# Attention and mixture of experts in one kernel: the experts' down products from one fp32 product to three float32r products of halves

## What is computed

```
xn  = layernorm(x)
out = x + attention(xn) + ffn(xn)

attention: 16 heads of 128, causal softmax, biases, output matrix, b_O
ffn:       x1 = xn + rotary_attention(rmsnorm(xn))      # 16 query heads, 4 key/value heads
           h  = rmsnorm(x1)
           p  = softmax(h @ gate.T); 4 of 32 experts by p + bias, their p made to sum to 1
           out = x1 + shared_expert(h) + sum over the chosen experts e of
                 w_e * ((silu(h @ weg[e]) * (h @ weu[e])) @ wed[e])
```

## Time and profile before

| what | value |
|---|---|
| median of 3 runs | 765.23 us (764.35 to 765.55) |
| profiled execution | 767.44 us |
| its span | 765.6 us |
| PE, DVE, ACT, POOL busy | 741.5, 543.1, 488.9, 476.4 us |

### The profile page before, as it was taken

How to read it: one execution, slowest core, us unless ns; L and a number is a source line. 1 busy time by engine, 2 the same in 40 slices (tenths; PEclk the granted TensorE clock), 3 DMA queues, 4 the chain that set the end, 5 groups by cost and what they waited for, 6 DMA issues and landing times. The chain is left out here.

```text
span 765.6 us, 14411 instructions
## 1 busy us (share of the span) xinstructions
PE 741.5 (97%) x4647; PEld 661.1 (86%) x4647; DVE 543.1 (71%) x1688; ACT 488.9 (64%) x1220; POOL 476.4 (62%) x550
## 2 busy tenths in 40 slices
PE   6799999999999999999989999999999999999997
PEld 3679898888889898989878989999989999999986
DVE  5888978797978887766698667555556565555574
ACT  3777777687777775677436665555656555666552
POOL 4757678686967685336355774466565856655553
PEclk9999999999999999999999999999999999999999
DMA  6001000000110099601002453476967876677634
GB/s 196 9 15 36 8 29 15 21 16 21 42 29 29 15 282 266 149 15 35 23 29 49 118 187 99 101 171 144 223 164 169 196 167 160 146 162 167 127 59 138
DMA packets 102691, 76.99 MB, mean 101 GB/s; under 512 B 6918, under 2 KB 101466, under 8 KB 102618
## 3 DMA queue, kind: packets, MB, share of 16 engines
q1 hardware_dynamic: 91426, 62.74, 29.4%
q0 software_dynamic: 10608, 12.61, 10.4%
q10 hardware_dynamic: 584, 0.73, 0.3%
HBM read 51.36 MB, written 24.69 MB: 99 GB/s over the span
## 5 line engine op out<-in xcount | busy, mean ns | idle before, releaser
L701 POOL TENSOR_SCALAR probs<-probs,inv_sum 128x128 f32<-128x128 f32 x240 | 141.2, 603 | 151.0 <-DVE inv_sum L1488 145.9
L1204 ACT ACTIVATE probs<-probs,neg_max 128x128 f32<-128x128 f32 (+3 forms) x256 | 143.0, 559 | 119.8 <-DVE neg_max L1482 118.6
L873 PE MATMUL s<-k_heads,q_heads 128*128 128x256 f32 (+2 forms) x576 | 137.9, 360 | 1.6 <-DVE neg_max L1482 1.2
L1482 DVE CUSTOM_DVE_ANT_0 probs<-s,mask 128x128 f32<-128x128 f32 (+3 forms) x256 | 120.0, 485 | 14.8 <-PE s L873 10.1
L763 POOL DMA_INDIRECT moe_sum_dram<-late,slot_tokens x63 | 99.2, 1574 | 40.9 <-ACT late L1292 27.8
L1497 DVE TENSOR_TENSOR probsT<-t,probsT 128x384 fp32r<-128x384 f32 (+2 forms) x192 | 101.2, 548 | 10.9 <-ACT probsT L1219 10.6
L1219 ACT ACTIVATE probsT<-t 128x384 fp32r<-128x384 f32 (+2 forms) x192 | 90.1, 487 | 17.9 <-PE t L1021 17.6
L873 PEld LDWEIGHTS s<-k_heads,q_heads 128*128 128x128 f32 x576 | 90.8, 190 | 7.8 <-DVE neg_max L1482 4.1
L1021 PE MATMUL t<-ident,probs 128*128 128x128 f32 x640 | 94.6, 274 | 2.8 <-POOL probs L701 2.1
L1021 PEld LDWEIGHTS t<-ident,probs 128*128 128x128 f32 x640 | 74.7, 140 | 12.4 <-POOL probs L701 4.1
L873 PE MATMUL zb<-probsT,v_heads 128*128 128x512 f32 (+2 forms) x351 | 69.3, 342 | 2.1 <-DVE probsT L1497 1.7
(11 more groups left out here) (262 smaller groups left out, 1582.0 us busy)
## 6 DMA issues: line engine op xcount, KB each, us to landing
x_slots_dram<-mask SPq DMA_DIRECT2D x1, 8480.0 KB, 41.4
late<-x_slots_dram SPq DMA_DIRECT2D x32, 265.0 KB, 4.7
late<-in_L_ffn_weg_dram SPq DMA_DIRECT2D x63, 128.0 KB, 3.1
late<-in_L_ffn_weu_dram SPq DMA_DIRECT2D x63, 128.0 KB, 3.1
late<-in_L_ffn_wed_dram SPq DMA_DIRECT2D x63, 128.0 KB, 3.5
moe_sum_dram<-mask SPq DMA_DIRECT2D x2, 1152.0 KB, 7.2
raw_qk<-in_L_ffn_wq_dram SPq DMA_DIRECT2D x16, 128.0 KB, 2.2
raw_o<-in_L_ffn_wo_dram SPq DMA_DIRECT2D x8, 256.0 KB, 2.7
```

What stands on the lines that cost most here:

```text
L701: pool.tensor_scalar(piece, piece, rinv[:, u % 2, i:i + 1], 1.0, ALU.mult, ALU.mult).then_inc(p_norm, 1)
L873: m = pe.matmul(dst, lhs(a), rhs(b), start=first and i == 0, stop=last_ and i == 2, skip_group_check=skip)
L1204: act.activation(piece, piece, ACT.Exp, bias=nmax[:, u % 2, i:i + 1], scale=-1.0, accum_out=rsum[:, u % 2, i:i + 1]).then_inc(e_done, 1)
L1482: ve.tensor_tensor_reduce(pr[:, u % 2, P_OFF[i]:P_OFF[i] + width], bS[i % 2][:, 0:width], mask_t[:, S - width:S], INV_SCALE, BIG, ALU.add, ...
```

## The change

Units 45 to 60 alone are changed. The down products of the expert pairs (not of the shared expert) go through `mm3`, on halves that are made new:

- `down_hi` (ACT) copies a pair's two down matrices, 512 columns, into the hi half of `ds`, and `down_lo` (DVE) subtracts for the lo half. Two of each a unit, one a pair.
- `inner_hi` (ACT) and `inner_lo` (DVE) do the same for the inner activations `hb`, both pairs of a unit in one instruction of 512 columns.
- PE's Y waits for the two lo halves and makes six float32r products of 256 columns for a pair.
- The shared expert's weights get a tile of their own, over whose place the new tiles `h_halves` and `w_down_halves` lie, and two constants move into the space that is free from the middle of the program on.

```diff
+        with ExitStack() as shared:
+            ws_t = shared.enter_context(nc.sbuf_tensor("w_shared", [P, KD * 2 * P + D], f32))
+        hs_t, ds_t = sb("h_halves", 2 * 4 * P, f32r), sb("w_down_halves", 2 * 4 * D, f32r)
...
+                else:
+                    r = ch[1]
+                    pe.wait_ge(dn_lo, r - SHARED + 1)
+                    pe.wait_ge(h_lo, (r - SHARED) // 2 + 1)
+                    for j in blocks_of(r):
+                        m = mm3(dst[:, j * D:(j + 1) * D], lambda p: hs[:, p, r % 2, j, :],
+                                lambda p: ds[:, p, r % 2, j * D:(j + 1) * D], j == 0, j == blocks_of(r)[-1], skip=True)
...
+            def down_hi(n, i):
+
+                for r in pairs_of(n)[i:i + 1]:
+                    if r >= SHARED:
+                        act.wait_ge(wr_in[(r - SHARED) % 3], 96 * ((r - SHARED) // 3) + 48 * len(blocks_of(r)))
+                        act.wait_ge(j_mm, CHUNK["Y", max(r - 2, SHARED - 1)] + 1)
+                        act.activation(ds[:, 0, r % 2, :], wdn[(r - SHARED) % 3].rearrange("p j d -> p (j d)"),
+                                       ACT.Copy).then_inc(dn_hi, 1)
+
+            def inner_hi(n):
+
+                rs = pairs_of(n)
+                if rs and rs[0] >= SHARED:
+                    kept(act, ("G", rs[0]))
+                    kept(act, ("G", rs[1]))
+                    act.activation(hs_t[:, 0:4 * P], hb_t, ACT.Copy).then_inc(h_hi, 1)
...
+            def down_lo(n, i):
+
+                for r in pairs_of(n)[i:i + 1]:
+                    if r >= SHARED:
+                        ve.wait_ge(dn_hi, r - SHARED + 1)
+                        ve.tensor_tensor(ds[:, 1, r % 2, :], wdn[(r - SHARED) % 3].rearrange("p j d -> p (j d)"),
+                                         ds[:, 0, r % 2, :].bitcast(f32), ALU.subtract).then_inc(dn_lo, 1)
+
+            def inner_lo(n):
+
+                rs = pairs_of(n)
+                if rs and rs[0] >= SHARED:
+                    ve.wait_ge(h_hi, (rs[0] - SHARED) // 2 + 1)
+                    ve.tensor_tensor(hs_t[:, 4 * P:], hb_t, hs_t[:, 0:4 * P].bitcast(f32), ALU.subtract).then_inc(h_lo, 1)
```

More of the change, by code:

```diff
@@ L247, in attention_pair_moe_kernel @@
         ident = sb("ident", P)
-        rows_t = sb("const_rows", P)
         cols_t = sb("const_cols", 64)
         gate_keep = sb("gate_cols", KD * E)
-        bO_t = sb("b_o", D)
         be_t = sb("bias_e", E)
@@ L273, in attention_pair_moe_kernel @@
         with ExitStack() as early:
-            accA_t, xrT_t, rope_t, t1_t, sw_t, vt_t = (
+            accA_t, xrT_t, rope_t, t1_t, sw_t, vt_t, rows_t, bO_t = (
                 early.enter_context(nc.sbuf_tensor(name, [P, cols], dt)) for name, cols, dt in (
                     ("acc_a", NT * D, f32), ("xrT", 2 * KD * NT * P, f32r), ("rope", 2 * S, f32),
-                    ("rope_sum", 3 * S, f32), ("rope_swapped", 2 * S, f32), ("vT", S, f32)))
+                    ("rope_sum", 3 * S, f32), ("rope_swapped", 2 * S, f32), ("vT", S, f32),
+                    ("const_rows", P, f32), ("b_o", D, f32)))
         PW = 2 * KD * 2 * P + 2 * D
-        late_t = sb("late", 2 * PW + 4 * P + 4 * ROW + KD * NT * P + KD * 2 * P + D + NT * ROW)
+        late_t = sb("late", 2 * PW + 4 * P + 4 * ROW + KD * NT * P + NT * ROW)
+        with ExitStack() as shared:
+            ws_t = shared.enter_context(nc.sbuf_tensor("w_shared", [P, KD * 2 * P + D], f32))
+        hs_t, ds_t = sb("h_halves", 2 * 4 * P, f32r), sb("w_down_halves", 2 * 4 * D, f32r)
         idx_t = sb("dest", NT * TOPK, i32)
@@ L289, in attention_pair_moe_kernel @@
         w0_t, w1_t, hb_t, xb_t = late(PW), late(PW), late(4 * P), late(4 * ROW)
-        x2T_t, ws_t, rows_t2 = late(KD * NT * P), late(KD * 2 * P + D), late(NT * ROW)
+        x2T_t, rows_t2 = late(KD * NT * P), late(NT * ROW)
         w2_t = rows_t2[:, 0:PW]
@@ L345, in attention_pair_moe_kernel @@
         sdn = ws_t[:, KD * 2 * P:]
+        hs = hs_t[:, :].rearrange("p (w s j c) -> p w s j c", w=2, s=2, j=2)
+        ds = ds_t[:, :].rearrange("p (w s c) -> p w s c", w=2, s=2)
         cws = cws_t[:, :].rearrange("p (s j) -> p s j", s=4)
@@ L407, in attention_pair_moe_kernel @@
         th_done, s_done, meta = sem("tanh_done"), sem("silu_done"), sem("slot_meta")
+        dn_hi, dn_lo, h_hi, h_lo = sem("w_down_hi"), sem("w_down_lo"), sem("h_hi"), sem("h_lo")
         y_out = [sem("y_scattered0"), sem("y_scattered1")]
@@ L977, in guest @@
                                                   stop=w == 1 and j == blocks_of(r)[-1] and k == KD - 1, skip_group_check=True)
-                else:
+                elif ch[1] < SHARED:
                     r = ch[1]
@@ L981, in guest @@
                     for j in blocks_of(r):
[L982 to L985, removed]
+                        m = pe.matmul(dst[:, j * D:(j + 1) * D], hb[:, r % 2, j, :], sdn, start=j == 0,
+                                      stop=j == blocks_of(r)[-1], skip_group_check=True)
+                else:
[5 more added lines that the diff above has]
+                                lambda p: ds[:, p, r % 2, j * D:(j + 1) * D], j == 0, j == blocks_of(r)[-1], skip=True)
                 m.then_inc(j_mm, 1)
@@ L1351, in step @@
                     normalise(n, (0, 1))
+                    down_hi(n, 0)
                     if nxt:
                         exp(n + 1, 2, it)
+                    down_hi(n, 1)
                     guests(n, 3)
@@ L1358, in step @@
                     normalise(n, (2,))
+                    inner_hi(n)
                     for ch in chs[:2]:
@@ L1645, in step @@
                     times_up(n, 3)
+                    down_lo(n, 0)
                     if nxt:
@@ L1652, in step @@
                     guests(n, 4)
+                    down_lo(n, 1)
+                    inner_lo(n)
                     route_m(n)
```

## The result

| | before | after |
|---|---|---|
| median of 18 runs each, taken together | 765.98 us (764.35 to 768.41) | 761.89 us (760.34 to 765.04) |
| ratio after / before | | 0.9949, 95% interval 0.9938 to 0.9960 |
| span of the profiled execution | 765.6 us | 760.0 us |
| from unit 45's start to unit 61's | 262.60 us | 257.36 us |

The account below looks back on a forecast made before the run. PE was taken as the bound in units 45 to 60. Products -4.7 us and unit 50's gap +0.45, halves and weights nothing, sum to -4.25: 761.0 us from a median of 765.23, range 759.2 to 764.0.

Parts of the forecast that it names:

- What bounds the kernel: Units 45 to 60: PE works without a gap but for one, so time taken from PE comes off the end time.
- Part 1, the products: Down products on PE: a pair goes from 0.87 to 0.72 us, 4.7 us off in all; bounds 7.2 off to 13.7 lost.
- Part 2, the halves: New copies on ACT and subtractions on DVE, 1.9 and 2.0 us a unit, fit into idle time and cost PE nothing.
- 1.05 us to spare: Unit 55: the last half is done at 650.4, and pair 24's down product needs it at 651.46.
- part 2 costs nothing on PE: Making the halves on ACT and DVE adds no PE time; without the cover each 0.1 us would cost 1.6 us.
- Part 3, the weights in time: Second weight copy on ACT: pair 25's load lands some 0.6 us ahead; cost nothing, at worst 0.1 us a unit.
- Part 4, the gap grows by 0.45 us: Unit 50: PE's wait for the slot rows' DMA grows, giving back 0.45 us; bounds nothing to 0.9 us.
- that row of issues keeps its length: SP's queue before unit 50: twenty-one DMAs issued one behind the other take as long as before, while PE is 0.45 us faster.
- The halves come late by a little: Rival: the halves exceed their spare by 0.15 us, PE waits that in each unit, 2.4 us in all, 763.4 us; chance 0.11.
- The gain is eaten: Rival: 0.27 us lost a unit, or float32r products of 145 ns, leave the time at 765.2 us; chance 0.07.
- the array is faster still: Rival: products on PE run at the lower bound, 6.5 us off in all, 758.7 us; chance 0.06.
- A lock between DVE and POOL: Rival: DVE's subtractions stand behind POOL's normalising and weight copies, PE waits 0.8 us a unit, 773.8 us; chance 0.06.

Follow-up runs that it names:

- the swap: Changed kernel with ACT's second weight copy moved behind the first pair's tanh; 788.81 us, ratio to the kernel before 0.9952, units 45 to 60 in 256.97 us.
- the swap with the edited queue: Changed kernel with that copy behind the tanh and ten attention-weight loads moved behind unit 50's slot rows on SP; 787.51 us, ratio to before 0.9928.

## Why the prediction was right, and where its steps failed

**What bounds the kernel: held.** PE's stretch shortened by 5.24 us and the span by 5.6.

**Part 1, the products: held to the digit.** The pair takes 0.72 us (forecast 0.72), the unit 16.15 (forecast 16.15), and 31.5 pairs give 4.7 us. The halves with the old products (261.86) against the swap (256.97) or the swap with the edited queue (256.87) give 4.9 and 5.0 us for the products, with unit 50's 0.17 us among it. The choice of the row of the same shape over both ends of its bounds was right. By the 109.2 ns of the Trainium skill (TensorE: Matmul & The Clock Gate, "Wait — 56ns, not 53.3ns?") the pair would have been an estimated 0.655 us; the chain of after has 120 ns for a product, each with its own weight load.

**Part 2, the halves: the place held, the spare did not.** ACT's new copies take 30.4 us by their durations (forecast 30), but its busy time is up by 21.5 only, since ACT instructions overlap their neighbours (by 0.1 us in the rows above) and the overlap counts once; DVE's subtractions take 39.2 us by their durations, its busy time is up by 31.9 (forecast 33), and the key's eviction starts 12.7 us into unit 55 (forecast 12.6). The step that failed is "1.05 us to spare" in unit 55: it was 0.64. Two things took it. The second weight subtraction was held for 0.34 us by POOL's normalising; it takes 1.02 or 1.03 us in fifteen of the sixteen units (1.20 in unit 52), and the kernel with POOL idle beside it has 0.68 us in its place. And ACT came into unit 55 late by the 0.35 us of the new wait. Where that wait is missing, in units 46, 47 and 49, the spare is 1.08 or 1.09 us with the same held subtraction, so there something made up for it: I had moved everything behind a copy by its duration, and an engine starts its next instruction earlier than that. In the rows above ACT's copy of 0.61 us starts at 641.37 and the tanh behind it at 641.88, 0.51 us later, and part of the rest is absorbed on the way: in unit 47 the first tanh stands 7.68 us into the unit (before 7.14, in unit 55) and the second 9.86 (before 9.48), so 0.54 and 0.38 us later where I had 0.65 for both. I listed who waits on PE for the delay of 0.65 us, but on POOL I followed only the normalising, not the addition behind it in the same queue. That is the real omission: the prediction's steps named the queue behind ACT's new instructions and left out the one behind POOL's. So "part 2 costs nothing on PE" held in the first profile with 0.05 us, though with no spare in two units, and failed in the two later ones (0.95 and 2.7 us). In the last unit the spare was 0.30 us (forecast 0.5).

**Part 3, the weights in time: held.** In the profile of after ACT never waits for a pair's weights. In the tightest case, in unit 59, the last transfer that the trace has is 0.13 us ahead of the copy's start; in unit 55 it is 2.3 us. So the tightest is less than the forecast 0.6, and nothing on PE came of it.

**Part 4, the gap grows by 0.45 us: wrong, with one half of it right.** The row of issues does start 0.45 us nearer to unit 50: 17.56 us ahead of it in all three profiles with the old products, 17.11 in that of after, and 17.10 or 17.11 in eight of the other ten with the new ones. But in the profile the gap shrank, from 0.96 to 0.42 us. The step that failed is "that row of issues keeps its length", together with the 4.77 us to the landing, which was taken as fixed. From the first issue of the earlier trace rows to the slot rows' issue it was 14.17 us before and 13.85 after, and from there to the landing 4.77 and 4.10; so 1.0 us was gained where 0.45 was lost, two thirds of it in the landing. The issues vary because single ones take 1.0 to 1.9 us in place of 0.4 to 0.6, and not the same ones each time. Unit 50 took 16.57, 18.26 and 17.33 us in three profiles of one kernel, with a wait for the slot rows in the first two only. One profile can't forecast such a term: its range was 0 to 0.9 and should have been -1 to 3.

**The sum.** -5.6 us of the profiled execution is -4.7, and -0.54 from part 4 with the other sign, -0.34 ahead of unit 45, where nothing is changed. The medians have -4.1. The 1.5 us between the two lie in the kernel before: its profiled execution (767.44) is 1.5 us above its own median, while that of after (761.80) is at its median (761.89). What the medians lack to the 4.7 us of the products is 0.6 us, within their interval (3.1 to 4.7 us). Late units and gaps as in the other profiles could be that; I have no profile of each run, and it is not shown. That -4.25 lies so close to -4.1 is in part luck: the 0.45 us that part 4 gives back is not what happened in the profile, and the losses of part 2 that other profiles show were put at nothing.

**The rivals.** "The halves come late by a little" is in part true: not in each unit, as it was put, but in one, three or six of the fourteen full units besides unit 50, with 0.05, 0.95 and 2.7 us in the three profiles, and by a mechanism the prediction didn't have. "The gain is eaten" by dearer products and "the array is faster still" are excluded by the chain's 0.72 us. "A lock between DVE and POOL": the lock is there, at the forecast place and only there in unit 55, with 0.34 us where I had put about 0.45. It doesn't decide the time by itself, since it needs 1.05 us or more. The Trainium skill (SBUF — State Buffer, "Who interferes with whom") says that a DVE instruction with two SBUF inputs contends with a GpSimd instruction that reads SBUF; the subtraction that goes from 1.03 to 0.68 us when POOL is idle agrees.

## What to carry to other kernels

On a bound engine, price a new product by a chain row of the same shape with the same weight loads; that was exact here. For work put on engines with idle time, follow the delay through each in-order queue it touches to the last instruction in it, DMAs included, and ask which buffer that DMA frees: the loss here came back a unit later, on another engine. Put a copy that only later work needs behind the step that others wait for, even where the profile shows no wait: it gave 0.36 us of spare in three undisturbed units.

## What the runs showed of the hardware

- Three float32r products of 256 columns take 0.36 us, and two fp32 records 0.435, with a weight load for each, at a granted clock of 1.00 (2.4 GHz).
- A subtraction of 512 columns with two SBUF inputs on DVE takes 0.68 us, and 1.02 to 1.07 beside POOL's TENSOR_SCALAR or TENSOR_TENSOR. Beside the normalising it came out alike, at 1.02 or 1.03 us, in fifteen of the sixteen units of after.
- Single DMA issues on SP's queue take 1.0 to 1.9 us where their neighbours take 0.4 to 0.6, at changing places. A wait for the slot rows' DMA behind some twenty of them varied from none to 1.9 us between profiles of one program; from its issue to its landing that DMA took 4.8 us before and 4.1 after.
- An indirect DMA that adds rows to memory, issued 13.1 us into the unit and waited for by ACT until 700.04, took at most 5.9 us from issue to landing; ACT waited 2.12 us for it.
